# Field-pair products and their sums on tiles of one shape, with the layers in the bank ring

## What is computed

```python
rows, cols = np.triu_indices(32, k=1)
p, q = e[:, rows, :], e[:, cols, :]
pij = jnp.einsum('bpe,dpe,bpd->bp', p, kernel, q)     # 496 numbers per row
z = pij @ W.T + b                                      # 256
h = jnp.concatenate([z, dense_ctx], axis=1)            # 272
h = jnp.maximum(h @ W_top1 + b_top1, 0.0)              # 512
h = jnp.maximum(h @ W_top2 + b_top2, 0.0)              # 256
y = h @ W_top3                                         # 1
```

## Time and profile before

| | |
|---|---|
| median of 3 runs | 860.19 us (859.13 to 860.83) |
| profiled execution, its own time | 859.6 us |
| its span, first to last instruction | 857.8 us |
| TensorE matmul busy | 829.0 us, 97% |
| VectorE busy | 616.9 us, 72% |
| ScalarE busy | 560.7 us, 65% |
| GpSimd busy | 472.2 us, 55% |
| HBM | 34 GB/s over the span |

### The profile page before, as it was taken

One profiled execution on the slowest core, in us unless ns is written; L12 is line 12 of the kernel. 1 busy time (PEld: TensorE's weight loads), 2 busy tenths in 40 slices (PEclk: granted clock), 3 DMA queues, 4 the chain that ended last, 5 costly groups with the idle time before them and its releaser, 6 DMA issues.

```text
span 857.8 us, 14292 instructions
## 1 busy us (share of the span) xinstructions
PE 829.0 (97%) x4104; PEld 289.5 (34%) x4104; DVE 616.9 (72%) x577; ACT 560.7 (65%) x4181; POOL 472.2 (55%) x502
## 2 busy tenths in 40 slices
PE   4999899999999999999999999999999999999998
PEld 1433233333333333333333333333333333333333
DVE  4478688888765766988765666888866775888850
ACT  0114698898716778898714777888822776888941
POOL 5777777777777777777777777777720000000000
PEclk9999999999999999999999999999999999999999
DMA  9911111111111111111111111111100000000000
GB/s 259 351 37 27 27 27 29 28 27 28 28 28 28 27 27 27 27 29 28 27 29 27 27 28 28 28 27 28 27 15 0 1 1 1 2 1 1 1 2 0
DMA packets 21621, 29.78 MB, mean 35 GB/s; under 512 B 10898, under 2 KB 11410, under 8 KB 20904
## 3 DMA queue, kind: packets, MB, share of 16 engines
q0 software_dynamic: 15872, 16.28, 9.8%
q1 hardware_dynamic: 3512, 9.84, 3.2%
q10 hardware_dynamic: 2160, 2.76, 1.2%
HBM read 28.85 MB, written 0.01 MB: 34 GB/s over the span
## 4 chain that ended last, share of the span: by engine, by line
PE 82%; POOL 7%; issue 5%; DVE 3%; ACT 2%; DMA 0%; DVEq 0%; SPq 0%; POOLq 0%
PE bilinear L692 36%; PE sums L732 19%; PE bilinear L704 13%; PE sums L763 8%; POOL emb_first L440 4%; POOL emb L440 3%; PE bilinear L670 3%; PE bilinear L763 2%; ACT batch_prod L525 1%; DVE batch_prod L603 1%; DVE prod L589 1%; DVE prod L592 1%; DVE prod L587 1%; DMA emb<-table,ids_sb 0%; DMA sums_sb<-dense_t 0%
## 5 line engine op out<-in xcount | busy, mean ns | idle before, releaser
L525 ACT ACTIVATE batch_prod<-batch_prod 128x64 f32<-128x64 f32 x2048 | 490.5, 241 | 98.9 <-DVE batch_prod L603 98.5
L592 DVE TENSOR_TENSOR prod<-bilinear,emb_t 128x1024 f32<-128x1024 f32 x352 | 414.9, 1216 | 123.2 <-PE bilinear L692 113.3
L440 POOL DMA_INDIRECT emb<-table,ids_sb x368 | 347.3, 944 | 112.2 <-issue 110.3
L692 PE MATMUL bilinear<-emb_t,k_sb 64*128 64x512 f32 x1536 | 389.4, 614 | 2.9 <-DVE prod L592 0.9
L525 ACT ACTIVATION_READ_ACCUMULATOR batch_prod<-batch_prod 128x1 f32 x2048 | 383.1, 187 | 0.0
L692 PEld LDWEIGHTS bilinear<-emb_t,k_sb 64*128 64x128 f32 x1536 | 131.4, 186 | 240.9 <-issue 115.5
L603 DVE TENSOR_TENSOR batch_prod<-bilinear,emb_first 128x1024 f32<-128x1024 f32 x128 | 155.7, 1216 | 46.3 <-PE bilinear L704 46.3
L732 PE MATMUL sums<-prod,pair_sel 128*32 128x512 f32 x1472 | 180.3, 600 | 1.1 <-DVE prod L589 1.1
L440 POOL DMA_INDIRECT emb_first<-table,ids_sb x128 | 124.2, 971 | 44.9 <-issue 37.3
L704 PE MATMUL bilinear<-k_sb,emb_t 64*128 64x512 f32 x512 | 138.2, 616 | 1.5 <-DVE prod L589 0.7
L484 ACT ACTIVATE emb_t<-bilinear 128x1024 f32<-128x1024 f32 (+1 forms) x40 | 33.8, 844 | 88.2 <-PE bilinear L670 81.5
(11 more groups left out here) (39 smaller groups left out, 139.6 us busy)
## 6 DMA issues: line engine op xcount, KB each, us to landing
emb<-table,ids_sb POOLq DMA_INDIRECT x368, 2.4
k_sb<-k_slots SPq DMA_DIRECT2D x2, 1088.0 KB, 21.6
emb_first<-table,ids_sb POOLq DMA_INDIRECT x128, 2.4
k_sb<-k_slots SPq DMA_DIRECT2D x1, 1600.0 KB, 23.0
k_sb<-k_slots SPq DMA_DIRECT2D x1, 1472.0 KB, 19.6
sums_sb<-looked_ids SPq DMA_DIRECT2D x1, 1024.0 KB, 10.2
k_sb<-k_slots SPq DMA_DIRECT2D x1, 960.0 KB, 14.8
k_sb<-k_slots SPq DMA_DIRECT2D x1, 896.0 KB, 24.8
```

The source lines that it names most:

```text
L440: nc.gpsimd.indirect_dma_start(fields_of(i, j, t)[:, f % 2, :], None, tables[f], bass.IndirectOffsetOnAxis(ap=ids_sb[:, start + t, f:f + 1 ...
L525: last = nc.scalar.activation(products, products, ACT.Copy, accum_out=batch_sums[:, t, row + f:row + f + 1])
L592: last = nc.vector.tensor_tensor(prod[:, at:at + 2, 0:n], bilinear[:, bank:bank + 2, 0:n], emb_t[:, j:j + 1, 0:n].to_broadcast([P, 2, n]), ...
L692: last = nc.tensor.matmul(bilinear[:, bank + row // EMB, 0:n], k_sb[row:row + EMB, operand, :], emb_t[row:row + EMB, double, 0:n], start=T ...
```

## The change

Slots, batches, look-ups and sums all run on tiles of 64x32: a slot or batch is two row halves by four column quarters, eight tiles; a quad takes the lower and the upper 64 partitions of four blocks apart, eight tiles, into both banks of `sums` at once, with a weight `row_sel` of one column of ones. So a group now holds 32 quads and fills both banks; there are two groups (32 quads; 14 quads and the joined batches), still four tensors of 128 rows in `sums_sb`. The first quad of a group waits until ScalarE has copied out both banks of the group before. `join` is a product with the identity on 128x32 tiles that adds to the banks; `batch_sums` has two halves and is cleared once. The pairs inside doubles are taken four doubles at a time, in one full slot with two blocks and four products of 64 partitions on VectorE; a chunk has 92 slots. There are no visits: a quad is due four units after its last slot, alone; turns are placed by slot numbers; a layer is placed after slots 10, 14, ..., 34 and takes a pair of the ring in every chunk. The batches come at slot 11 + 2.3n (17 + 2.3n in chunk 0). The dense inputs take eight DMAs into groups 2 and 3 of `sums_sb` and wait for all four copies; the gathers' counts are 40 and 4.6.

```diff
@@ -46,7 +46,7 @@
 for _m in range(1, DOUBLES):
     OPERANDS += [(_m, _j) for _j in range(_m)]
     if _m % 4 == 3:
-        OPERANDS += [(_m - 2, None), (_m, None)]
+        OPERANDS.append((_m, None))
 NOPERANDS = len(OPERANDS)
...
@@ -60,52 +60,48 @@
 BLOCKS = []
 for _m, _j in SLOTS:
     SLOT_BLOCK.append(len(BLOCKS))
-    BLOCKS += [(_m, None, 0)] if _j is None else [(_m, _j, 0), (_m, _j, 1)]
+    BLOCKS += [(_m, _j, 0), (_m, _j, 1)]
...
-GROUP_QUADS = 16
+GROUP_QUADS = 32
+HALVES = 2
 QUARTER = 32
 NGROUPS = -(-NQUADS // GROUP_QUADS)
 
-PHASE = 2
-assert NQUADS % PHASE == 0 and GROUP_QUADS % PHASE == 0
-
 RING = 3
-SUM_LAG = 3
+SUM_LAG = 4
...
+FIRST_LAYER = 10
+LAYER_EVERY = 4
...
-TURNS_EARLY = {20: 0, 21: 2, 22: 4}
-TURNS = {1: 6, 4: 8, 6: 10, 10: 12, 13: 14}
-LAYER_VISITS = (0, 2, 3, 5, 7, 8, 9)
...
-FIRST_BATCH_FROM, FIRST_BATCH_EVERY = 18, 2.4
-BATCH_FROM, BATCH_EVERY = 12, 2.45
+TURNS_EARLY = {84: 0, 87: 2, 90: 4}
+TURNS = {8: 6, 17: 8, 27: 10, 40: 12, 54: 14}
...
+FIRST_BATCH_FROM, FIRST_BATCH_EVERY = 17, 2.3
+BATCH_FROM, BATCH_EVERY = 11, 2.3
...
+BATCHED_AT = NQUADS - (NGROUPS - 1) * GROUP_QUADS
+BATCHED_ROWS = BATCHED // (HALVES * 4)
+SPARE_AT = BATCHED_AT + BATCHED_ROWS
...
     if j is None:
-        return (2 * m, 2 * m + 1), (2 * m - 2, 2 * m - 1)
+        low, high = within_doubles(m, half)
+        return (2 * low, 2 * low + 1), (2 * high, 2 * high + 1)
     return (2 * j, 2 * m + half), (2 * j + 1, 2 * m + half)
...
@@ -226,17 +211,24 @@
             turned = max(turned, needed + 1)
         steps.append((kind, i, which))
         if kind == "slot":
-            visits += [(at + SUM_LAG, visit(i, v)) for v in range(NQUADS // PHASE)
-                       if last_slot_of_quad((v + 1) * PHASE - 1) == which]
+            quads = [q for q in range(NQUADS) if last_slot_of_quad(q) == which]
+            sums += [(at + SUM_LAG, ("sum", i, q)) for q in quads]
+            if which == NSLOTS - 1:
+                sums.append((at + SUM_LAG + 1, ("join", i, 0)))
+            if i > 0 and which in TURNS:
+                steps.append(("turn", i, (TURNS[which], 2)))
+            if i + 1 < NCHUNKS and which in TURNS_EARLY:
+                steps.append(("turn", i + 1, (TURNS_EARLY[which], 2)))
+            k = (which - FIRST_LAYER) // LAYER_EVERY
+            if i > 0 and (which - FIRST_LAYER) % LAYER_EVERY == 0 and 0 <= k < NOUTS:
+                steps.append(("layer", i - 1, k))
         else:
-            reduces += [(at + REDUCE_LAG * (half + 1), ("reduce", i, (*which, half))) for half in range(2)]
+            reduces += [(at + REDUCE_LAG * (half + 1), ("reduce", i, (*which, half))) for half in range(HALVES)]
         while reduces and reduces[0][0] <= at:
             steps.append(reduces.pop(0)[1])
...
-    for _, late in visits:
-        steps += late
+        while sums and sums[0][0] <= at:
+            steps.append(sums.pop(0)[1])
+    steps += [step for at, step in reduces] + [step for at, step in sums]
     steps += [("layer", NCHUNKS - 1, k) for k in range(NOUTS)]
     return steps
 
@@ -244,8 +236,7 @@
 PROGRAM = program()
 
 
-RING_USES = [step for step in PROGRAM
-             if step[0] in ("slot", "batch", "turn") or (step[0] == "layer" and step[1] == NCHUNKS - 1)]
+RING_USES = [step for step in PROGRAM if step[0] in ("slot", "batch", "turn", "layer")]
...
@@ -404,10 +384,10 @@
 
             for i in range(NCHUNKS):
                 at = CHUNKS[i][0] * P
-                sp.wait_ge(s_sums_out, i * NSUMS + DENSE_GROUP + 1)
-                for b in range(4):
-                    row = 32 * b + SPARE_AT
-                    sp.dma_start(sums_sb[row:row + SPARE, DENSE_GROUP, 0:cols(i)],
+                sp.wait_ge(s_sums_out, (i + 1) * NSUMS)
+                for b in range(8):
+                    row = 32 * (b % 4) + SPARE_AT
...
@@ -485,19 +465,19 @@
                                      ACT.Copy).then_inc(s_emb_t, 1)
 
             def group_out(i, g):
-                if g < NGROUPS:
-                    act.wait_ge(s_summed, i * NQUADS + min(GROUP_QUADS * (g + 1), NQUADS))
+                if g < NGROUPS - 1:
+                    act.wait_ge(s_summed, i * NQUADS + GROUP_QUADS * (g + 1))
                 else:
                     act.wait_ge(s_joined, i + 1)
 
-                if i > 0:
-                    act.wait_ge(s_layer, (i - 1) * NOUTS + (H1_OUTS if g == 0 else NOUTS))
-                nc.scalar.activation(sums_sb[:, g, 0:cols(i)], sums[:, g % 2, 0:cols(i)],
-                                     ACT.Copy).then_inc(s_sums_out, 1)
+                wait(act, s_layer, i * NOUTS)
+                for half in range(HALVES):
+                    nc.scalar.activation(sums_sb[:, g * HALVES + half, 0:cols(i)], sums[:, half, 0:cols(i)],
+                                         ACT.Copy).then_inc(s_sums_out, 1)
 
             def layer_out(i, k):
                 n = cols(i)
-                source = layer_bank(i, k)[:, 0:n]
+                source = bilinear[:, ring_bank("layer", i, k), 0:n]
                 act.wait_ge(s_layer, i * NOUTS + k + 1)
...
@@ -565,7 +547,7 @@
             nc.vector.tensor_tensor(b_comb_sb[:], bilinear[:, NSUMS, 0:H1 // P], b1_sb[:], ALU.add).then_inc(s_folded_out, 1)
             for at, g in enumerate(reversed(range(NSUMS))):
                 dve.wait_ge(s_folded, at + 2)
-                if g == DENSE_GROUP:
+                if g >= NSUMS - HALVES:
...
@@ -584,10 +566,11 @@
                 wait(dve, s_summed, quad - PROD_QUADS + 1)
                 dve.wait_ge(s_bilinear, g + 1)
                 if j is None:
-                    nc.vector.tensor_tensor(prod[EMB:P, at, 0:n], bilinear[EMB:P, bank, 0:n],
-                                            emb_t[EMB:P, m - 1, 0:n], ALU.mult)
-                    last = nc.vector.tensor_tensor(prod[0:EMB, at, 0:n], bilinear[0:EMB, bank + 1, 0:n],
-                                                   emb_t[0:EMB, m, 0:n], ALU.mult)
+
+                    for half, by in enumerate((slice(EMB, P), slice(0, EMB))):
+                        for rows, double in zip((slice(0, EMB), slice(EMB, P)), within_doubles(m, half)):
+                            last = nc.vector.tensor_tensor(prod[rows, at + half, 0:n], bilinear[rows, bank + half, 0:n],
+                                                           emb_t[by, double, 0:n], ALU.mult)
                 else:
...
@@ -687,11 +673,13 @@
                 operand = OPERANDS.index((m, j))
                 row_ready(("slot", i, s))
                 ring_free("slot", i, s)
-                low = m if j is not None else m - 1
-                for row, double in ((0, low), (EMB, m)):
-                    last = nc.tensor.matmul(bilinear[:, bank + row // EMB, 0:n], k_sb[row:row + EMB, operand, :],
-                                            emb_t[row:row + EMB, double, 0:n], start=True, stop=True,
-                                            tile_position=(row, 0))
+                for row in (0, EMB):
+                    for col in range(0, P, QUARTER):
+                        double = m if j is not None else within_doubles(m, row // EMB)[col // EMB]
+                        last = nc.tensor.matmul(bilinear[col:col + QUARTER, bank + row // EMB, 0:n],
+                                                k_sb[row:row + EMB, operand, col:col + QUARTER],
+                                                emb_t[row:row + EMB, double, 0:n], start=True, stop=True,
+                                                tile_position=(row, col))
...
                 for row in (0, EMB):
-                    last = nc.tensor.matmul(bilinear[:, bank + row // EMB, :],
-                                            emb_t[row:row + EMB, m, t * P:(t + 1) * P],
-                                            k_sb[row:row + EMB, operand:operand + len(BATCH_DOUBLES), :],
-                                            start=True, stop=True, tile_position=(row, 0))
+                    for col in range(0, P, QUARTER):
+                        last = nc.tensor.matmul(bilinear[col:col + QUARTER, bank + row // EMB, :],
+                                                emb_t[row:row + EMB, m, t * P + col:t * P + col + QUARTER],
+                                                k_sb[row:row + EMB, operand:operand + len(BATCH_DOUBLES), :],
+                                                start=True, stop=True, tile_position=(row, col))
...
-            def sum_bank(i, g):
-
-                wait(pe, s_sums_out, i * NSUMS + g - 1)
-                if i > 0 and g in (1, 2):
-                    pe.wait_ge(s_layer_out, (i - 1) * NOUTS + max(k for k in range(NOUTS) if idle_bank(k) == g % 2) + 1)
-                return g % 2
-
             def join(i):
 
                 pe.wait_ge(s_reduced, 2 * BATCHES_TO[i + 1])
-                bank = sum_bank(i, NGROUPS)
-                for t in range(CHUNKS[i][1]):
-                    last = nc.tensor.transpose(sums[:, bank, t * P:(t + 1) * P], batch_sums[:, t, :], ident[:])
```

(43 more changed lines are left out.)

101 lines of the change are left out of this document (40 added, 61 removed).

## The result

The changed kernel takes 824.32 us (median of 4 runs, 823.46 to 825.15) where the kernel before takes 859.66 (4 runs beside it): ratio 0.9593, 95% interval 0.958 to 0.9606. The forecast was 819.6 us, range 800 to 843. The profiled execution took 825.15, its span 823.4.

What follows compares the result with a forecast made beforehand. TensorE, busy 97% of the span, was taken as the bound, stretched by tile-shape changes and VectorE ring waits. 859.6 - 37.8 (three chunks) - 7.4 (chunk 0) + 4.6 (tail) = 819.0; median 819.6 us, range 800 to 843.

Steps and rivals of the forecast that it cites:

- Steps 1 and 4: Slots, batches and sums on 64x32 tiles: 23 shape changes per chunk go, 7.8 us; eight tiles cost a pass nothing.
- The sequencer-bound rival: TensorE's sequencer paces its load and MATMUL pairs: at 71 ns a pair, 1010 us, slower; chance 0.03.
- the passes that don't overlap: Rival on TensorE: eight-tile passes last 0.454 us instead of 0.429, giving 887 us, slower; chance 0.06.
- Step 3: One quad after every two slots lets VectorE catch up: most of 9.4 us of ring waits per chunk goes.
- waits for products nearly gone in the first 35 slots: Sign expected in the profile: TensorE hardly waits for VectorE's products in that part of a chunk.
- Step 2: Within-double pairs: eight half-empty slots per chunk become four full ones, 3.4 us less; VectorE's work for them stays.
- The coupling of three engines: Slots 35 to 83: TensorE, ScalarE and VectorE won't all run full; 5 us a chunk, between bounds of nothing and 9.
- The near-tie: Slots 35 to 83: TensorE 83.5 us, ScalarE 83.8, VectorE 82.4, within 2% of each other.
- Quad 0 after the join: The next chunk's first quad, one slot after the join, waits 0.6 us for ScalarE's evictions of the sum banks.
- Chunks starting 188 us apart: Sign expected in the profile: a chunk takes 188.2 us, 12.6 less than 200.8.
- ScalarE's line: From turn 11 to chunk 1: 92.2 us of batches, 5, 6.5 and 3.3 for coupling make 107.0, against 111.6 before.
- The tail: After the last quad: eight dense-row DMAs wait for the last eviction, T + 20.7 instead of T + 16.1, 4.6 us lost once.

## Why the prediction was right, and where it was off

- Steps 1 and 4, the tile shape and eight tiles at 0.429 us a pass: right. The changes of shape were worth 6.9 us in chunk 3 where 7.8 stood. The sequencer-bound rival and the passes that don't overlap fell with the first timeline. On the other chips the count of instructions does matter, by a mechanism that no rival had. The 62 ns a MATMUL that the Trainium skill ("TensorE: Matmul & The Clock Gate", section "Wait — 56ns, not 53.3ns?") gives for hardware decoding switched off do not appear on the first chip: a unit has one MATMUL per 54 ns and keeps 0.86 us. Which way of decoding ran, no run here shows.
- Step 3, single quads: the direction right, the size off. I took most of 9.4 us for it; undone, it costs 2.9. With pairs there is no wait before quad 32 and with single quads there is one of 2.7, so half of what the ring waits took comes back as a wait for ScalarE. The sign that I named, waits for products nearly gone in the first 35 slots, did not show either, for the reason in the next point.
- Step 2, within-double slots, was the term that failed. "VectorE's work for them stays" was true, but in one slot the four products hold a single ring pair for 2.8 us. In chunk 2 the stands behind it were 1.8 at slot 22, 1.3 at slot 45, 0.8 at slot 8 and 0.3 at slot 2: 4.2 us where I had zero (some 0.3 of it is the usual way into a layer and a turn). Removing them gave 4.2 in chunk 3.
- The coupling of three engines: 5 us assumed, with some 2 at quad 32. In the trace it is all at quad 32: 2.7 of standing and 1.7 of clock (in all, what four passes at 0.85 instead of 0.43 lose), 4.4 together. Apart from the within-double slot 44, units elsewhere in that stage go at 0.858. From slot 35 to 83 chunk 1 took 88.9 us, where 83.5 and 5 stood, and ScalarE was busy 83.9 of them (94%; over 90% forecast). The near-tie was real, but three buffers carried it to the one place where TensorE must wait for ScalarE.
- Quad 0 after the join: 0.6 expected, 0.4 measured. Chunks starting 188 us apart were the sign; chunk 2 took 191.3, chunk 3 190.2 to the last quad.
- Chunk 1 took 195.2: double 7 of chunk 1 landed at 231.5, as GpSimd issues a double per 10.0 us in chunk 1 as well. I had applied to chunk 0 only. Starting chunk 1 earlier met the gathers: 1.5 us of standing and another fall of the clock.
- Chunk 0: turn 11 came at 112.79 (113.0 forecast); from there to chunk 1 it took 101.0, not 107.0. TensorE's own 100.6 was the bound; ScalarE's line, which I took, wasn't, and there was no wait of a layer in it, and one of 0.4 us for a late gather.
- The tail: 3.9 us lost (4.6 forecast), by the mechanism named: eight DMAs behind the last eviction. From its end to TensorE's going on it takes 3.6 us, where 4.2 stood.
- The errors cancel in part, and that is luck: +7 in chunk 1, +3 and +3 in chunks 2 and 3 (held against what each took before), -6 in chunk 0, -0.7 in the tail. That is the 6 us between 819.0 and 825.15 for the profiled execution. The median is 4.7 off, as it lies 0.8 below the profiled execution where I had put it 0.6 above.

## What to carry to other kernels

Give all products that alternate on TensorE one tile shape first; only then does it pay to interleave them finely, since each switch is gone. When a ring of a few buffers is shared, ask of every use how long it holds its buffer, not how much work it makes in all: four short products in one use stalled TensorE for up to 1.8 us, where the uses of two products before left it idle for 0.3 at most. When a tuned kernel gets faster, look for every supply with a fixed pace (here gathers of 10.0 us a double) in all stages, and count instructions: three times as many on TensorE were free on one chip and cost some 15 ns each, the lower clock that came with it included, on others. The gain of 4% on one chip was a loss of 16% on another.
